# A graph-network kernel on one core: how the edge stage sums messages into nodes

## What is computed

```
m_input  = concatenate([x[src], x[dst], edge_attr])         # 128 + 128 + 64 features per edge
h        = relu(m_input @ W1 + b1)
messages = relu(h @ W2 + b2)
agg      = segment_sum(messages, dst, num_segments=N)       # edges -> nodes
x        = layernorm(x + relu(agg @ Wn + bn)) ...
```

## Time and profile before

| | us |
|---|---|
| median of 3 runs | 2293.29 (2291.87 to 2295.23) |
| span of the profiled execution | 2166.6 |
| what lies around that span (difference of the two) | 126.7 |
| last edge window added, from the start of the span | 1832.5 |
| PE busy, whole span | 1892.6 (87%) |
| PEld busy | 1536.6 (71%) |
| DVE busy | 863.9 (40%) |
| POOL busy | 767.3 (35%) |
| ACT busy | 647.7 (30%) |

### The profile page before, as it was taken

The page is one execution under the profiler, slowest core; times in us unless marked ns, Lnnn a source line. Parts: engine busy times, 40 slices in busy tenths (PEclk is TensorE's granted clock), DMA queues, the critical chain, the costliest instruction groups (busy, mean ns, idle before and its releaser), DMA issues.

```text
span 2166.6 us, 36842 instructions
## 1 busy us (share of the span) xinstructions
PE 1892.6 (87%) x11147; PEld 1536.6 (71%) x11148; DVE 863.9 (40%) x2898; ACT 647.7 (30%) x1217; POOL 767.3 (35%) x805
## 2 busy tenths in 40 slices
PE   3777779989878888889999999999999997797796
PEld 2444454445577777779999999999999997444344
DVE  7998860123333333333333333333333332745203
ACT  4666650010023333332222222222222221610201
POOL 3000000000047777776555555555555552100000
PEclk9999979999979999995555555555555555899898
DMA  1000000010143333332222222222222222000001
GB/s 48 0 0 0 0 2 1 0 34 0 36 120 82 82 79 81 82 81 65 61 60 59 60 59 59 60 60 60 60 59 58 59 60 62 1 4 1 2 1 30
DMA packets 158346, 93.70 MB, mean 43 GB/s; under 512 B 120530, under 2 KB 143825, under 8 KB 158297
## 3 DMA queue, kind: packets, MB, share of 16 engines
q0 software_dynamic: 25088, 51.43, 8.7%
q1 hardware_dynamic: 133208, 41.60, 7.9%
HBM read 86.44 MB, written 6.52 MB: 43 GB/s over the span
## 4 chain that ended last, share of the span: by engine, by line
PE 51%; DMA 9%; issue 4%; DVE 4%; POOL 3%; ACT 1%; DVEq 1%; SPq 1%; POOLq 0%; ACTq 0%
PE ps L846 11%; PE ps L831 10%; PE ps L855 9%; DMA arena<-x_w1a,idx 8%; PE ps L724 7%; PE ps L823 5%; PE ps L839 5%; POOL arena L605 3%; PE ps L921 2%; DVE arena L1316 1%; DVE idx L1430 1%; DMA x_w1b<-arena 0%; DVE stats L1306 0%; PE ps L931 0%; PE ps L952 0%
## 5 line engine op out<-in xcount | busy, mean ns | idle before, releaser
L605 POOL DMA_INDIRECT arena<-x_w1a,idx x784 | 740.3, 944 | 1054.9 <-issue 781.8
L724 PE MATMUL ps<-adj,arena 128*128 (+2 forms) x1875 | 367.6, 358 | 14.3 <-DVE arena L1281 7.9
L846 PE MATMUL ps<-w_c,arena 128*128 128x128 f32 x1568 | 345.9, 390 | 0.0
L855 PEld LDWEIGHTS ps<-arena 128*128 128x128 f32 x1568 | 297.9, 282 | 58.8 <-ACT arena L1109 56.8
L855 PE MATMUL ps<-arena 128*128 128x24 f32 x1568 | 293.4, 334 | 41.0 <-ACT arena L1109 41.0
L1109 ACT ACTIVATE arena<-arena 128x512 f32<-128x512 f32 x196 | 123.4, 629 | 671.1 <-DVE arena L1465 671.1
L831 PE MATMUL ps<-arena 88*128 88x128 f32 x1568 | 321.9, 375 | 1.6 <-DMA arena<-x_w1b 0.9
L724 PEld LDWEIGHTS ps<-adj,arena 128*128 128x128 bf16 x1875 | 172.0, 99 | 203.1 <-issue 25.9
L831 PEld LDWEIGHTS ps<-arena 88*128 88x128 f32 x1568 | 305.2, 288 | 2.4 <-ACT arena L1100 2.4
L846 PEld LDWEIGHTS ps<-w_c,arena 128*128 128x128 f32 x1568 | 304.8, 288 | 0.4 <-ACT arena L1105 0.4
L1460 DVE TENSOR_TENSOR arena<-ps,arena 128x512 f32<-128x512 f32 x196 | 135.6, 692 | 356.9 <-DMA arena<-x_w1a,idx 225.6
(11 more groups left out here) (165 smaller groups left out, 1252.7 us busy)
## 6 DMA issues: line engine op xcount, KB each, us to landing
arena<-in_edge_attr SPq DMA_DIRECT2D x196, 128.0 KB, 2.3
arena<-x_w1a,idx POOLq DMA_INDIRECT x784
arena<-x_w1b SPq DMA_DIRECT2D x196, 12.0 KB
x_spill<-arena SPq DMA_DIRECT2D x1, 1600.0 KB, 7.8
x_w1a<-arena SPq DMA_DIRECT2D x6, 256.0 KB, 2.3
x_w1b<-arena SPq DMA_DIRECT2D x6, 256.0 KB, 2.5
arena<-x_spill SPq DMA_DIRECT2D x6, 256.0 KB, 4.6
out_x<-arena SPq DMA_DIRECT2D x3, 512.0 KB
```

Of the source, the lines that this page charges most:

```text
L605: pool.indirect_dma_start(out=z_e[v][:, j * D:(j + 1) * D], out_offset=None, in_=xa_d[:, :], in_offset=bass.IndirectOffsetOnAxis(ap=idx[:, ...
L724: last = pe.matmul(ps[:, u, 0:w], parts[q][:, k, :], adj[:, k, bass.ds(c0, w)], start=(k == 0 and q == 0), stop=(k == NT - 1 and q == 2))
L846: last = pe.matmul(ps[:, 5 + v % 2, j * P:(j + 1) * P], h_t[v % 2][:, j * P:(j + 1) * P], w_c[:, :], start=True, stop=True)
L855: last = pe.matmul(ps[:, 7, 0:WIN], msg[v % 2][:, j * P:(j + 1) * P], oh_e[v][:, j, :], start=(j == 0), stop=(j == J - 1))
```

## The change

It does the following, in the edge stage only:

- Step 5 is done with operands exchanged. `sum_nodes` takes the one-hot of a tile, widened to `SWIN` = 32 columns, as the stationary operand and the 128 columns of messages as the moving one. The four tiles of a block write to four different quarters of the partitions of one bank (`ps[32j:32j+32, 1, 0:D]`), each with start and stop.
- ACT copies this bank to SBUF (`take_sums`), and one more matmul (`window`) multiplies it by `fold`, a 128 by 24 matrix of stacked identities: this adds the four quarters and transposes the result to 128 features by 24 nodes, as `add_window` needs it. DVE adds it one step later than before.
- The bank for `sum_nodes` is taken from the transposed inputs, which had banks 0 and 1 in turn and now have bank 0 alone.
- All hand-overs between engines use one counting semaphore instead of four by slot. In the loop the awaited value is then 4i + v + 1.

```
-                for j in range(J):
-                    last = pe.matmul(ps[:, 7, 0:WIN], msg[v % 2][:, j * P:(j + 1) * P], oh_e[v][:, j, :],
-                                     start=(j == 0), stop=(j == J - 1))
-                last.then_inc(win_ready[v], 1)
+            def sum_nodes(i, v):
+                passed(pe, msg_ready, i, v)
+                passed(pe, oh_e_ready, i, v)
+                passed(pe, sums_out, i, v, back=1)
+                for j in range(J):
+                    last = pe.matmul(ps[SWIN * j:SWIN * (j + 1), 1, 0:D], oh_e[v][:, j, :],
+                                     msg[v % 2][:, j * P:(j + 1) * P], start=True, stop=True)
+                last.then_inc(sums_ready, 1)
+
+            def window(i, v):
+                passed(pe, sums_out, i, v)
+                passed(pe, win_added, i, v, back=1)
+                pe.matmul(ps[:, 7, 0:WIN], sums[v % 2], fold[:, :], start=True, stop=True).then_inc(win_ready, 1)
...
             def step(i, v, first=False, left=2):
...
                 if not first:
+                    sum_nodes(*at(i, v - 1))
+                messages(i, v)
+                if not first:
                     window(*at(i, v - 1))
-                messages(i, v)
...
-                passed(pe, ect_out, i, v, back=2)
+                passed(pe, ect_out, i, v, back=1)
                 for j in range(J):
-                    last = pe.transpose(ps[0:KE, v % 2, j * P:(j + 1) * P], ec[v % 2][:, j, :], ident_f[:, :])
+                    last = pe.transpose(ps[0:KE, 0, j * P:(j + 1) * P], ec[v % 2][:, j, :], ident_f[:, :])
...
+            def take_sums(i, v):
+                passed(act, sums_ready, i, v)
+                passed(act, win_ready, i, v, back=2)
+                act.activation(sums[v % 2], ps[:, 1, 0:D], ACT.Copy).then_inc(sums_out, 1)
...
                 hidden_relu(i, v)
                 if left >= 2:
                     inputs_out(*at(i, v + 2))
+                if not first:
+                    take_sums(*at(i, v - 1))
                 message_relu(i, v)
...
-                    add_window(*at(i, v - 1), b)
+                    add_window(*at(i, v - 2), b)
...
-        def passed(eng, sems, i, v, back=0, by=1):
+        def passed(eng, s, i, v, back=0, by=1):
             w = v - back
-            n = by * (i + 1) if w >= 0 else by * i
-            wait_from_one(eng, sems[w % SLOTS], n)
+            if isinstance(s, list):
+                n = by * (i + 1) if w >= 0 else by * i
+                wait_from_one(eng, s[w % SLOTS], n)
+            else:
+                n = SLOTS * i + w + 1
+                if not (isinstance(n, int) and n <= 0):
+                    eng.wait_ge(s, n)
```

More of the change, by code:

```diff
@@ L95, in build @@
         idx = sb("idx", [P, SLOTS, J], I32)
-        win_i = sb("win_i", [P, WIN], F32)
+        win_i = sb("win_i", [P, SWIN], F32)
+        fold = sb("fold", [P, WIN], F32)
         off = sb("off", [P, 9], F32)
@@ L211, in build @@
         ec_loaded = [sem(f"ec_loaded{v}") for v in range(SLOTS)]
-        ec_onehot = [sem(f"ec_onehot{v}") for v in range(SLOTS)]
-        ec_used = [sem(f"ec_used{v}") for v in range(SLOTS)]
+        ec_onehot = sem("ec_onehot")
+        ec_used = sem("ec_used")
         w_loaded = [sem(f"w_loaded{v}") for v in range(SLOTS)]
[L215 to L225, removed]
+        oh_e_ready = sem("oh_e_ready")
+        ect_out = sem("ect_out")
+        z_ready = sem("z_ready")
+        z_sum = sem("z_sum")
+        zt_ready = sem("zt_ready")
+        h_ready = sem("h_ready")
+        m_ready = sem("m_ready")
+        m_sum = sem("m_sum")
+        msg_ready = sem("msg_ready")
+        sums_ready = sem("sums_ready")
+        sums_out = sem("sums_out")
+        fold_ready = sem("fold_ready")
+        win_ready = sem("win_ready")
+        win_added = sem("win_added")
         g_loaded = [sem(f"g_loaded{v}") for v in range(SLOTS)]
-        idx_ready = [sem(f"idx_ready{v}") for v in range(SLOTS)]
+        idx_ready = sem("idx_ready")
         gather_mark = sem("gather_mark")
@@ L601, in gather @@
                 passed(pool, idx_ready, i, v)
-                wait_from_one(pool, zt_ready[v], i)
+                passed(pool, zt_ready, i, v, back=SLOTS)
                 pool.sem_inc(gather_mark, 1)
@@ L884, in _ @@
                     step(NB // SLOTS - 1, v, left=SLOTS - 1 - v)
+                sum_nodes(NB // SLOTS - 1, SLOTS - 1)
                 window(NB // SLOTS - 1, SLOTS - 1)
@@ L1121, in _ @@
                 inputs_out(0, 1)
-                for v in range(SLOTS):
-                    step(0, v)
+                step(0, 0, first=True)
+                for v in range(1, SLOTS + 1):
+                    step(*at(0, v))
                 with act.Fori(1, NB // SLOTS - 1) as i:
-                    for v in range(SLOTS):
-                        step(i, v)
-                for v in range(SLOTS):
+                    for v in range(1, SLOTS + 1):
+                        step(*at(i, v))
+                for v in range(1, SLOTS):
                     step(NB // SLOTS - 1, v, left=SLOTS - 1 - v)
+                take_sums(NB // SLOTS - 1, SLOTS - 1)
             phase_end(act, 6)
@@ L1494, in _ @@
                 step(0, 0, first=True)
+                step(0, 1)
                 b = bases(dve, base_regs, 0)
-                for v in range(1, SLOTS + 1):
-                    step(*at(0, v), b[v - 1])
+                for v in range(2, SLOTS + 1):
+                    step(*at(0, v), b[v - 2])
                 with dve.Fori(1, NB // SLOTS - 1) as i:
-                    b = bases(dve, base_regs, i)
+                    b = bases(dve, base_regs, i, v0=-1)
                     for v in range(1, SLOTS + 1):
                         step(*at(i, v), b[v - 1])
-                b = bases(dve, base_regs, NB // SLOTS - 1)
+                b = bases(dve, base_regs, NB // SLOTS - 1, v0=-1)
                 for v in range(1, SLOTS):
                     step(NB // SLOTS - 1, v, b[v - 1], left=SLOTS - 1 - v)
-                add_window(NB // SLOTS - 1, SLOTS - 1, b[SLOTS - 1])
+                b = bases(dve, base_regs, NB // SLOTS - 1)
+                for v in range(SLOTS - 2, SLOTS):
+                    add_window(NB // SLOTS - 1, v, b[v])
             phase_end(dve, 6)
```

48 lines of the change are left out of this document (27 added, 21 removed).

## The result

The changed kernel takes **2351.61 us** (median of 4 executions, 2347.51 to 2358.37), the kernel before beside it 2292.58 us (2290.12 to 2295.23). The ratio is 1.0243, with a 95% interval of 1.0216 to 1.027: it is slower by 59 us. The forecast was 2070, and the range ended at 2190.

The account below looks back on a forecast made before the run. Bound: POOL at 5.00 us a block first, then PE at half clock, 6.83. Restoring POOL's pace gives −217 us, the tail −6: span 2166.6 to 1943.6, plus 126.7 around it, 2070 us; range 2054 to 2190.

Parts of the forecast that it names:

- The 126.7 us around it, which I leave as they are: Outside the profiled span: 126.7 us taken as unchanged and added to the predicted span of 1943.6 us.
- A fall then ends after a few us: PE's clock in the edge stage: with narrow work shrunk and the period changed, falls to 1.2 GHz end quickly.
- the 10 us that the prediction had set as its own limit: Sign in the edge stage: a half-clock stretch of more than some 10 us means the clock step is wrong.
- I priced falls at nothing: Clock falls in the edge stage cost 0 us, since gathers run ahead of their use.
- The stage stays at POOL's pace: Edge stage: 5.00 us a block throughout; 493 gathers take 616 us instead of 833, −217 us.
- the upper bound: sum_nodes on PE: four quarter products one after another, 0.9 us at full clock; all at once would be 0.22.
- The copy and its hand-over are covered: ACT's copy before the fold: hidden behind messages, 0.9 us; without that cover up to 0.5 us on PE.
- Semaphores and the single bank: nothing: Counting semaphores taken as 0, at worst 10 us; inputs in one bank cause no wait.
- B: Rival, edge stage: clock stays at half, quarters run one after another; 2346 us, up to 2450; chance 0.11.
- D: Rival: sum_nodes plus fold cost just 1.71 us, clock stays at half, nothing changes; 2293 us; chance 0.04.
- A: Rival, edge stage: clock stays at 1.2 GHz, quarters side by side, 5.97 us a block; 2187 us; chance 0.09.
- C: Rival, edge stage: clock returns but falls for long stretches, or PE partly bounds; 2130 to 2210 us; chance 0.13.

Follow-up runs that it names:

- b_again: The kernel before, unchanged, run again to see its usual execution: 2293.19 us, ratio 1.0015.
- w48: Kernel before with the moving one-hot of the window product widened from 24 to 48 columns: 2276.22 us, ratio 0.9933.
- tiny8: Kernel before with eight more two-column products a block ahead of the window product: 2300.72 us, ratio 1.0041.
- one_gather: Kernel before issuing one gather of the four in each block, other engines doing all their work: 1666.5 us.
- after_one_gather: Changed kernel issuing one gather of the four in each block: 1662.64 us.
- the early copy: DVE's index copy moved to the start of its step, ahead of its waits; on the changed kernel 1940.65 us (6 runs).
- relay: Changed kernel's order, bank, semaphores, ACT copy and last product (by an identity), but node sums formed as before: 2383.86 us, ratio 1.0393.
- experiment 5: Kernel before with one gather, two gathers or four plain transfers a block: 1666.5, 1708.05, 1668.15 us; changed kernel with one gather: 1662.64 us.
- two_gathers: Kernel before issuing two gathers of the four in each block: 1708.05 us.
- experiment 6: Kernel before with one gather and three iota writes a block, keeping POOL busy: 1925.54 to 1931.42 us five times, 2083.9, 2103.39, 2263.87.
- keep_busy: Kernel before with five float32 products of 128 columns into unused columns ahead of each block's node sums: 2316.42 us, ratio 1.0107.
- early_index: Kernel before with DVE's index copy moved ahead of its waits: 1940.19, 1940.23, 1942.28, 2101.18, 2148.94 and 2249.78 us; unmoved beside it 2145.63.
- experiment 9: DVE's index copy moved ahead of its waits: kernel before 1940.19 to 2249.78 us over six runs, changed kernel 1940.65 us.
- experiment 1: The kernel before, unchanged, run again to test whether its shown profile was usual: 2293.19 us, ratio 1.0015.

## Why the prediction was wrong

**"The 126.7 us around it, which I leave as they are": wrong.** Spans end 1.8 us under the times (2345.7 and 2347.51 after, 2291.0 and 2292.78 in `b_again`). I set the span of one execution against the median of others and took the difference for something outside the kernel. It was the blocks at POOL's pace that the usual execution does not have, some 70 of them: 70 × (6.74 − 5.00) = 122 us. The span of 2166.6 beside three times of 2292 to 2295 should have told that the execution on the page was another kind.

**"A fall then ends after a few us": half right.** No stretch of hundreds of us at 0.50 is left. Most falls last 3 to 10 us, but eleven of 14 to 21 us stand between the first gather and the last, over the 10 us that the prediction had set as its own limit. And they come back at once: I priced falls at nothing from a stage that stood at half clock for a tenth of the time, and here it is half. That the narrow products held the clock down is not shown either: `w48` widens them and ends the long stretches, but `tiny8` leaves them and does so too. Nor do the transposes hold it down by themselves: `one_gather` has them all, and its clock is 1.00 for 500 us.

**"The stage stays at POOL's pace": the step that failed, with 2.06 us × 196 blocks = 404 us.** I took two states, full clock at 5.00 us and half clock at 6.83, and concluded from the clock to the pace. There is a third: the clock going up and down, PE's completions several us late, POOL waiting for its index (231.8 of 800 us). The falls alone do not make the pace. A block takes PE 3.55 us at 1.0 (`after_one_gather`) and 6.44 at 0.5 (in this trace, from the L857 at 1308.65 to that at 1315.09); with half of the time at each I estimate 4.6 us a block, under POOL's 5.00. Measured are 7.06. In kernels of before's form the late way takes about what half clock takes (6.69 to 6.90 us a block), so the gain in clock brought nothing. How the lateness reaches POOL is read from the waits: a late product holds DVE, DVE's index copy stands behind that wait, and POOL's gathers wait for the copy. No run takes away the lateness alone. With the 404 us the forecast of the span, 1943.6, becomes 2348, and the span is 2345.7. What the changed program takes where the stage does stay at POOL's pace is near the forecast: 1937.2 with the early copy.

**The quarters: the upper bound was the wrong choice, and it did not matter.** The prediction counted from start to start. So counted, with PE the bound at full clock, `after_one_gather` and `one_gather` have (start, duration):

```profile
1002.12 0.43 PE L867 MATMUL ps<-arena 128*32 128x128 f32 x8
1002.53 1.16 PE L857 MATMUL ps<-w_c,arena 128*128 128x128 f32 x8
1003.53 0.30 PE L875 MATMUL ps<-fold,arena 128*128 128x24 f32 x2
1003.67 1.14 PE L842 MATMUL ps<-arena 88*128 88x128 f32 x8
```

```profile
1002.46 0.97 PE L855 MATMUL ps<-arena 128*128 128x24 f32 x8
1003.27 1.14 PE L846 MATMUL ps<-w_c,arena 128*128 128x128 f32 x8
```

The node sums take 0.41 us where I took 0.9, and the fold 0.14 where I had 0.22; L855 took 0.81. The way into the quarters costs little: from the last transposes to the node sums it is 0.53 us there and 0.44 in `one_gather` (medians of 800 to 1300 us). PE's block is 3.5 us, not 3.8. At PE's own pace both forms are equal within 4 us (1662.64 and 1666.5).

**"The copy and its hand-over are covered": wrong in the late way.** With POOL the bound it would be so. In the late way the change adds a hand-over a block that can meet a late completion of PE, the one to ACT's copy: ACT waits there on "remote" for 106.1 of 800 us, and PE in turn waits for the copy. `relay` prices the whole way at 92 us, 0.47 us a block (that these waits are what it pays for is argued, not shown); I had named "up to 0.5 us on PE" as the price without the cover, and then counted none. Semaphores and the single bank: nothing, as I said.

**The rivals.** B's 2346 is 6 us from the result, by luck: it had the clock at 0.50 and PE as the bound, and neither holds. D and A did not come. C was nearest in kind, as the clock does return and keeps falling; but it lost POOL's pace in half of the blocks behind the first fall and through the clock alone, while the whole stage lost it, and not through the clock alone.

**What stays open.** Why PE's completions come late, and what starts and ends it. All 12 executions in which POOL was done before PE (experiment 5, on two chips) lie below 1711 us, and their four traces have it not at all or, in `two_gathers`, barely. POOL slower than PE allows it and does not force it (experiment 6). It is not the bytes moved, the number of products, the quarters, the semaphores, or five more products on PE. That idle time of PE starts it would fit experiments 5 and 6; `keep_busy`, built on that thought, stayed slow, but left PE idle at its waits. Whether the early copy keeps the stage out of it, or only met a favourable hour, is open too; `early_index` at POOL's pace three times of six, beside a before that was there once in 11, does not settle it.

## What to carry to other kernels

Before any sum, compare the span of the profiled execution with the times of the others: here a gap of 5% was another way of running the same program, and its calm half no promise of the usual one. A granted clock at its upper level does not prove progress, and a mean of 0.75 can be an alternation of two levels; look at when the waiting engines start (waits that end on nothing the profile knows), and count blocks per 100 us. Where one engine paces a loop through several others, it is worth trying to take the cheap instruction that feeds it, here an index copy of 0.17 us, out from behind the waits for slow results; experiment 9 does not prove its worth.

## What the hardware showed that was not expected

- Two slow forms with one pace: clock 0.50 and PE busy 100 of 100 us, 58 gathers; clock 0.70 and PE busy 77 us, 60 gathers (experiment 1).
- PE at full clock for 500 us without a fall when it is never left waiting (1.00, 500.00 busy).
- Four products in four partition quarters overlap: eight passes in a row of 0.43 us, as against eight of `messages` in 1.14 to 1.35 us; from start to start 0.41 us, where the four 24-column products took 0.81.
- In the late way most late completions stand where the granted clock is 1.0 (71% of the updates there over 0.5 us late in the changed kernel, against 25% at 0.5).
- Moving 48 instead of 24 columns, work for nothing, made a kernel faster by 0.67% [0.44, 0.91].
- One program on one chip between 1943 and 2255 us in 11 executions, with the mean clock from 0.941 to 0.708.
